# Cross attention of a decoder layer: stacked key and query parts by way of DRAM, folded weights split in the self phase

## The reference

```python
def proj(x, W, bias):
    y = x @ W.T + bias
    y = y.reshape(b, s, H, dk, M)
    return jnp.transpose(y, (0, 2, 1, 3, 4))
qh, kh, vh = proj(q, Wq, bq), proj(k, Wk, bk), proj(v, Wv, bv)
def interfere(x):
    return x + 0.1 * amp[0] * jnp.einsum('bhsdi,hij->bhsdj', x, interference)
qh, kh, vh = (interfere(qh), interfere(kh), interfere(vh))
scores = jnp.einsum('bhqdm,bhkdm->bhqkm', qh, kh) / math.sqrt(dk)
weights = jax.nn.softmax(scores, axis=3)        # over the 4 slots m
out = jnp.einsum('bhqkm,bhkdm->bhqdm', weights, vh)
return out.transpose(0, 2, 1, 3, 4).reshape(b, s, dm) @ Wo.T + bo
...
x = x + self_attention(layernorm(x))
x = x + cross_attention(layernorm(x), ctx, ctx)
x = x + ffn(layernorm(x))
```

## Time and profile before

| | us |
|---|---|
| median of 3 runs | 3619.1 (3616.62 to 3624.29) |
| the profiled execution's own time | 3618.95 |
| its span in the trace | 3616.8 |
| cross phase in the trace | about 2036 to 3272 |
| mean granted clock | 0.977 |

### The profile page before, as it was taken

One profiled execution on the slowest core, in us unless ns is written; L12 is line 12 of the kernel. 1 busy time (PEld: TensorE's weight loads), 2 busy tenths in 40 slices (PEclk: granted clock), 3 DMA queues, 4 the chain that ended last, 5 costly groups with the idle time before them and its releaser, 6 DMA issues. The chain is left out here.

```text
span 3616.8 us, 49438 instructions
## 1 busy us (share of the span) xinstructions
PE 3440.5 (95%) x18100; PEld 2677.0 (74%) x18100; DVE 1494.1 (41%) x2238; ACT 1185.0 (33%) x1679; POOL 1250.3 (35%) x563
## 2 busy tenths in 40 slices
PE   6999999999999999999999679989979999998999
PEld 5888887888878888878787467767767777763587
DVE  3232332323332232423232446656656665652453
ACT  3232232323233232323222235445444454440110
POOL 4334343434324343434342334434334443320000
PEclk9999999999999999999999889999999999999999
DMA  4323233323333232332221254544555455534032
GB/s 168 106 94 113 89 135 130 115 93 106 127 128 117 93 110 93 128 134 89 85 93 53 108 150 128 173 146 137 156 152 137 129 161 162 141 88 157 35 133 76
DMA packets 137253, 431.16 MB, mean 119 GB/s; under 512 B 24112, under 2 KB 24112, under 8 KB 137144
## 3 DMA queue, kind: packets, MB, share of 16 engines
q1 hardware_dynamic: 131384, 408.58, 35.1%
q10 hardware_dynamic: 5760, 20.97, 1.4%
HBM read 316.21 MB, written 37.75 MB: 98 GB/s over the span
## 5 line engine op out<-in xcount | busy, mean ns | idle before, releaser
L446 POOL TENSOR_TENSOR sa_wl<-sa_wraw,sa_wh 128x1024 fp32r<-128x1024 f32 x192 | 458.2, 2402 | 777.3 <-ACT sa_wh L597 777.3
L53 PE MATMUL sa_u<-sa_ln_xh,sa_wh 128*128 128x512 f32 x1536 | 628.5, 409 | 4.4 <-DVE sa_ln_xl L254 4.4
L54 PE MATMUL sa_u<-sa_ln_xl,sa_wh 128*128 128x512 f32 x1536 | 599.7, 390 | 0.0
L55 PE MATMUL sa_u<-sa_ln_xh,sa_wl 128*128 128x512 f32 x1536 | 599.3, 390 | 0.0
L457 POOL TENSOR_TENSOR sa_pl<-sa_praw,sa_ph 128x1024 fp32r<-128x1024 f32 x128 | 318.0, 2516 | 446.4 <-ACT sa_ph L649 446.4
L53 PE MATMUL sa_pr<-sa_ph,sa_oh 128*128 128x512 f32 x1024 | 428.6, 419 | 0.1
L746 DVE TENSOR_TENSOR sa_acc<-sa_pr,sa_acc 128x512 f32<-128x512 f32 x256 | 176.9, 692 | 569.3 <-PE sa_pr L55 569.3
L54 PE MATMUL sa_pr<-sa_pl,sa_oh 128*128 128x512 f32 x1024 | 400.8, 391 | 0.0
L55 PE MATMUL sa_pr<-sa_ph,sa_ol 128*128 128x512 f32 x1024 | 400.0, 391 | 0.0
L738 DVE TENSOR_TENSOR sa_ol<-sa_o,sa_oh 128x512 fp32r<-128x512 f32 x128 | 88.6, 692 | 718.5 <-ACT sa_oh L661 718.5
L53 PEld LDWEIGHTS sa_u<-sa_ln_xh,sa_wh 128*128 128x128 f32 x1536 | 289.3, 188 | 83.6 <-issue 24.2
(11 more groups left out here) (185 smaller groups left out, 5765.7 us busy)
## 6 DMA issues: line engine op xcount, KB each, us to landing
sa_wraw<-in_wqkv SPq DMA_DIRECT2D x192, 512.0 KB, 3.5
sa_praw<-in_wproj SPq DMA_DIRECT2D x128, 512.0 KB, 3.5
ca_wraw<-w_folded SPq DMA_DIRECT2D x96, 512.0 KB, 3.2
ca_kstack<-ca_kmh SPq DMA_DIRECT2D x256, 128.0 KB, 2.4
ca_wraw<-in_wo SPq DMA_DIRECT2D x33, 512.0 KB, 4.2
ca_kstack<-ca_kml SPq DMA_DIRECT2D x128, 128.0 KB, 2.4
ca_qstack<-ca_qh SPq DMA_DIRECT2D x256, 64.0 KB, 2.5
sa_nat<-in_w_nat SPq DMA_DIRECT2D x24, 512.0 KB, 4.7
```

What stands on the lines that cost most here:

```text
L53: nc.tensor.matmul(out, ah, bh, start=(first and i == 0), stop=False)
L54: nc.tensor.matmul(out, ah, bl, start=False, stop=False)
L55: ins = nc.tensor.matmul(out, al, bh, start=False, stop=(last and i == len(parts) - 1))
L446: nc.gpsimd.tensor_tensor(wl[:, u % 3], wraw[:, u % 3], f32(wh[:, u % 3]), ALU.subtract).then_inc(w_split, 1)
```

## The change

Four things change.

1. In the self phase, ACT writes the high part `sa_foldh`, DVE subtracts the low part `sa_foldl` in two new instructions per steady step (24 steps), and ACT stores two tiles, `w_folded_hi` and `w_folded_lo`. The softmax's semaphores become one, `soft_steps`.
2. In the cross phase, SP loads K, Q and V weights straight into `ca_wh` and `ca_wl`. ACT's copies and POOL's subtractions for them go; only OUT is still split (`ca_owraw`, ACT, POOL).
3. `mask_k` goes. SP stores `kh`, `kl`, `qh` and `ql` to DRAM (`k_parts`, `q_parts`, 256 KB each), waits for the store, and loads back: six key DMAs (`stack_keys`, 16 partitions x 4 x 512, 128 KB each) and three query DMAs (`stack_queries`, 32 partitions x 4 x 512, 256 KB each). Rows of the other head in `ca_kstack` are zeroed once, by a memset of 8192 columns on POOL at the start of the phase.
4. `pairmask` and `slotmask` leave the constants (three POOL instructions, one on DVE).

The diff, cut to its core:

```diff
@@ constants_phase
-            pool.memset(slotmask[:], 1.0).then_inc(masks_built, 1)
...
-            nc.vector.tensor_reduce(pairmask[:], slotmask[:].rearrange("p (r w) -> p w r", w=2), AX.X,
                                     ALU.add).then_inc(mix_steps, 1)
@@ self_attention_phase, ACT and DVE
-                        act.wait_ge(fold_stored, m * 16 + 16)
-                    nc.scalar.activation(fold[:, half * HALF:(half + 1) * HALF], v_ps[:], ACT.Copy
-                                         ).then_inc(v_copied, 1)
+                        act.wait_ge(fold_stored, m * 32 + 32)
+                    nc.scalar.activation(foldh[:, half * HALF:(half + 1) * HALF], v_ps[:], ACT.Copy
+                                         ).then_inc(fold_hi, 1)
...
-                    act.dma_start(tile_of(w_folded, m), fold[:]).then_inc(fold_stored, 16)
+                    act.dma_start(tile_of(w_folded_hi, m), f32(foldh[:])).then_inc(fold_stored, 16)
+                    act.dma_start(tile_of(w_folded_lo, m), f32(foldl[:])).then_inc(fold_stored, 16)
...
+                def low_fold(half):
+                    if not s.steady:
+                        return
+                    dve.wait_ge(fold_hi, m * 2 + (half + 1))
+                    cols = slice(half * HALF, (half + 1) * HALF)
+                    nc.vector.tensor_tensor(foldl[:, cols], v_ps[:], f32(foldh[:, cols]), ALU.subtract
+                                            ).then_inc(v_copied, 1)
...
                 low_o(0)
                 next_moments(0)
+                low_fold(0)
                 low_o(1)
                 next_moments(1)
                 add_projected(0)
+                low_fold(1)
@@ cross_attention_phase, SP
+            def weights(u, g):
+                first = CH * WHICH[u]
+                sp.dma_start(f32(wh[:, u]), tile_of(w_folded_hi, g + first)).then_inc(w_loaded[u], 16)
+                sp.dma_start(f32(wl[:, u]), tile_of(w_folded_lo, g + first)).then_inc(w_loaded[u], 16)
+
+            def next_weights(s, u):
+                if s.nxt:
+                    sp.wait_ge(u_done, s.n * U + (u + 1))
+                    weights(u, s.next_g)
...
-            def stack(dst, a, part, stacked):
-
-                for r in range(PAIRS):
-                    sp.dma_start(f32(dst[a * PC:(a + 1) * PC, r]), f32(part[r * PC:(r + 1) * PC])
-                                 ).then_inc(stacked, 16)
+            def stack_keys(par, a, part):
+                by_slot = part.rearrange("(r w d) n -> w d r n", w=2, d=DK)
+                for w in range(2):
+                    rows = slice(a * PC + w * DK, a * PC + (w + 1) * DK)
+                    sp.dma_start(f32(kstack[rows, par, :, w]), by_slot[w]).then_inc(k_stacked, 16)
+
+            def stack_queries(a, part):
+                sp.dma_start(f32(qstack[a * PC:(a + 1) * PC]), part.rearrange("(r p) n -> p r n", p=PC)
+                             ).then_inc(q_stacked, 16)
...
                 if s.proj:
-                    sp.wait_ge(km_ready, s.n * 2 + 1)
-                    stack(kstack[:, s.par], 0, kmh, k_stacked)
-                    stack(kstack[:, s.par], 2, kmh, k_stacked)
-                    sp.wait_ge(km_ready, s.n * 2 + 2)
-                    stack(kstack[:, s.par], 1, kml, k_stacked)
-                    weights(s.n + 1, OUT, s.g, 0 if s.nxt else 2)
+                    sp.wait_ge(ow_split, s.n + 1)
+                    sp.dma_start(owraw[:], tile_of(wo, s.g)).then_inc(owraw_loaded, 16)
+                    sp.wait_ge(u_hi, s.n * 2 + 1)
+                    sp.dma_start(k_parts[0], f32(kh[:])).then_inc(k_hi_stored, 16)
+                    sp.wait_ge(u_free, s.n * U + 3)
+                    sp.dma_start(k_parts[1], f32(kl[:])).then_inc(k_lo_stored, 16)
+                    sp.wait_ge(kstack_zeroed, 1)
+                    sp.wait_ge(k_hi_stored, s.n * 16 + 16)
+                    stack_keys(s.par, 0, k_parts[0])
+                    stack_keys(s.par, 2, k_parts[0])
+                    sp.wait_ge(k_lo_stored, s.n * 16 + 16)
+                    stack_keys(s.par, 1, k_parts[1])
+                    next_weights(s, 0)
                     sp.wait_ge(u_hi, s.n * 2 + 2)
+                    sp.dma_start(q_parts[0], f32(qh[:])).then_inc(q_hi_stored, 16)
+                    sp.wait_ge(u_free, s.n * U + 4)
+                    sp.dma_start(q_parts[1], f32(ql[:])).then_inc(q_lo_stored, 16)
                     if s.attn:
                         sp.wait_ge(s_done, s.m * TILES + TILES)
-                    stack(qstack, 0, qh, q_stacked)
-                    stack(qstack, 1, qh, q_stacked)
-                    sp.wait_ge(u_free, s.n * U + 4)
-                    stack(qstack, 2, ql, q_stacked)
-                    if s.nxt:
-                        weights(s.n + 1, VALUE, s.next_g)
+                    sp.wait_ge(q_hi_stored, s.n * 16 + 16)
+                    stack_queries(0, q_parts[0])
+                    stack_queries(1, q_parts[0])
+                    sp.wait_ge(q_lo_stored, s.n * 16 + 16)
+                    stack_queries(2, q_parts[1])
+                    next_weights(s, 1)
                 if s.norm:
                     load_context(s.b + 1, range(CRAW, KC))
+                if s.proj:
+                    next_weights(s, 2)
@@ cross_attention_phase, POOL
+            nc.gpsimd.memset(f32(kstack[:]), 0.0).then_inc(kstack_zeroed, 1)
             nc.gpsimd.memset(v[:], 0.0).then_inc(v_set, 1)
...
-            def mask_k(s):
...
             def step(s):
-                weights(s.n, OUT, 0 if s.proj else 2)
-                if s.proj:
-                    weights(s.n, VALUE)
-                    mask_k(s)
-                if s.nxt:
-                    weights(s.n, KEY)
-                    weights(s.n, QUERY)
+                out_weights(s)
```

## The result

The changed kernel takes 3635.3 us (median of 6 runs, 3631.66 to 3638.53) against 3617.9 for the kernel before in the same sessions: a ratio of 1.0046, 95% interval 1.0033 to 1.006. It is slower by some 17 us. The profiled execution is the shortest of the six, 3631.66 us with a span of 3629.9, 13.1 us longer than the span before.

What follows compares the result with a forecast made beforehand. PE, busy 95%, was taken to bound the kernel, so only its waits could change. Constants -0.5, self phase 0, start -12.5 and steady steps +9 gave -4 from 3618.95: 3615 us, range 3602 to 3633 (forecast's own 3611 to 3626).

Steps and rivals of the forecast that it cites:

- Steady steps: Cross phase: the query chain behind the low half makes PE 0.35 us late in 26 places, +9 us (0 to +24).
- window of 190 GB/s: Earlier trace: one of two rates, 212 and 190 GB/s, read for pieces into 32 partitions with full queues.
- The start: Start of the cross phase: PE's 18.2 us wait for a query stack shrinks, -12.5 us (-8 to -16).
- The third rival: The gap at the start shrinks less, -8 instead of -12.5, giving 3619 us; included in the forecast's 0.43 chance.
- Weights "at nothing": Cross phase: loading 1 MB instead of 512 KB per unit, into queues busy 0.49 of the step, costs nothing.
- The constants: Kernel start: three POOL instructions and one on DVE leave the chain, -0.5 us, at most the 2.24 us wait.
- the memset: Start of the cross phase: zeroing `ca_kstack` starts PE some 1.4 us later, swallowed by its 6.80 us normalise wait.
- Step 0: First step of the cross phase: ends at the same time, 2084.3, or up to 2 us earlier.
- The self phase: Two more DVE subtractions and a store in each of 24 steady steps, taken as 0 (0 to +1.6).
- The keys: Steady cross steps: key stacks end early, starting 16.7 us ahead of the low query half; cost nothing.
- The sum: Whole kernel: -0.5 + 0 - 12.5 + 9 = -4, so 3615 us.
- the slower rival: Steady cross steps: nothing in the query chain overlaps, 0.93 us late in 26 places, +24; 3630 us, chance 0.22.

Runs made afterwards that it cites:

- that part alone: The kernel before with only key and query halves stored to DRAM and loaded back stacked, without masks; 3640.2 us, 1.0058 of before.
- The weights' part alone: The changed kernel with masks and stacking within SBUF as before, leaving only folded weights split in the self phase; 3611.2 us, 0.9977 of before.

## Why the prediction was wrong

**Steady steps: the step that failed.** The mechanism was named, with its 26 places, and the price was bounded by 0 and 0.93 us. I chose 0.35, "near the overlapped value, since the order of the queue is fixed but start-ups overlap". The scores begin 5.9 to 7.0 us after the low half, 6.47 in the mean of the 26 places, where 6.5 was worked out for a full queue and 5.85 for an overlapped one: the start-ups gave next to nothing. Against the 5.57 of before that is 0.90 late; PE's recorded wait is 0.73 of it, and a plain steady step became 0.86 longer. Over the 26 places the term was +9, and 26 x 0.90 is +23, at its upper end of +24. Moving the high stacks out of the chain took the waits in the steady steps away, and 17 us, so the size belongs to this term. One reading behind the price was off as well: in the window of 190 GB/s a weight load of 512 KB (issued at 2087.40, landed at 2099.14) was in the queue with the query pieces, so that rate isn't one of pieces alone.

**The start: smaller than forecast, and wrong in its cause.** -12.5 was forecast. The first scores came 12.2 us earlier, but 2.9 of that lay ahead of the cross phase, where two executions of the same program differed by 4.9; so the near agreement is luck, and the cross phase's own gain is 9.3. And I put it down to the key stacks by way of DRAM; that part alone left 16.2 of 18.2 us. The weights' part alone won 7.6. What held the start was SP, in its waits for weight splits, so that the key pieces went out behind them and behind 2 MB of accumulators. The trace of the kernel before has it, one row ahead of the pieces whose times I read (timeline, three weight issues that took SP 13.22 us, then the accumulators):

```profile
2063.12 13.22 SPq L911 DMA_DIRECT2D ca_wraw<-w_folded  x3
...
2076.39 1.93 SPq L915 DMA_DIRECT2D ca_acc<-x  x4
```

The third rival (the gap doesn't shrink as said) was right for the stacks and wrong for the sum.

**Weights "at nothing": wrong.** The queue had room on average (0.49 of a step), and the loads still cost where something urgent stood behind them: the next block's x in the norm steps, and with it `ca_o`. The steps around the block changes lost 8.8 us. On the version with queries within SBUF, where they had lost 1.8, loading V later made them 1.6 shorter than before, 3.4 us of the 5.6 that the medians show.

**What held.** The constants gave 0.4 (8.0 to 7.6; forecast 0.5). PE's first wait in the cross phase grew from 12.0 to 13.4 with the memset. Step 0 ended 49.0 us after the self phase, where it was 47.6 before; with the weights' part, which has no such memset, it was 48.8, so there is no sign that the memset cost time. The self phase shows no new wait of PE. The keys were early in steady steps. Their loads into 16 partitions ran at 151 GB/s with the queues full, below the 190 to 212 of the earlier trace rows, and decided nothing here. The Trainium skill (SBUF — State Buffer, "Door 1: The DMA port swizzle") gives 104 GB/s for 16 partitions; the trace lies in the direction of its rule and not at its full size.

**The sum.** In the cross phase the trace has -9.3 up to the first scores, -0.2 in the step behind them, +18.0 in the plain steady steps and +8.8 around the block changes: +17, the slower rival's side. That rival was right in its place and in its lateness (0.93, measured 0.90). Its price of 3630 stopped short of the measured 3635.3, since it had the full gain at the start and nothing for the block changes.

## What to carry to other kernels

When a transfer is sent by way of DRAM, count the chain behind the last part that is produced, not the bytes: store, completion and load back each waited here for what was queued before them, so take every part that is ready earlier out of that chain, and price it as fully queued unless the trace shows overlap. When a waiting queue engine stands ahead of a gap, find out which of its waits holds it before giving the gain to the step that follows. And a queue that is half empty on average can still hold up the one urgent load behind it.

## What the runs showed of the hardware

A jump back to the head of a long loop body cost PE a wait of 9.5 us in the kernel before and of 8.6 to 11.6 in the other looped versions, with the DMA engines at a busy share of 0.97 to 1.04 meanwhile. Written out, the same work ran through without that gap, and two kernels came out 25 and 26 us shorter for two jumps; in their traces 17.5 and 23.5 of it stand around the jumps. In the run with 256 KB more into 32 partitions PE waited 1.6 to 1.9 us (once 2.8) ahead of every steady step; in nine of 21 the granted clock of the next four microseconds was 0.57 to 0.61, in the others 1.00. An extra 256 KB in a query chain cost 1.0 us into 32 partitions and 0.74 into 128, closer to each other than the 212 and 406 GB/s of the earlier trace rows would have it; why, is open.
